# Softmax attention on one core: the negated row maxima as twelve more rows of the second scores' operands

## The reference, cut to what matters

```python
h = tok(x)                                  # embedding, 6 dilated causal convolutions, log-softmax
h = h + attn(layernorm(h), Q, E)            # causal linear attention, no softmax
h = h + ffn(layernorm(h), ...)              # the block below, B=8 sequences, T=256 rows, C=64
# in ffn: NH = 4 query heads, NKV = 2 key/value heads, HD = 16
q, k = rope(h @ wq.T), rope(h @ wk.T)
scores = einsum('bhtd,bhsd->bhts', q, k) / sqrt(HD)
scores = where(causal, scores, -1e30)
att = softmax(scores, axis=-1)
y = einsum('bhts,bhsd->bhtd', att, v)
x = x + y @ wo.T
# then rmsnorm, a router over 8 experts (top 2) and the experts' silu(x w1) * (x w3) @ w2
```

## Time and profile before

| what | value |
|---|---|
| median of 3 runs | 255.79 us (255.70 to 256.33) |
| profiled execution, its own time | 255.79 us |
| its span (first to last instruction) | 254.1 us |
| PE, DVE, ACT, POOL busy | 86%, 71%, 64%, 63% of the span |
| granted TensorE clock | 1.00 throughout |
| softmax attention, 118 to 172 us | PE 45.1, DVE 41.7, ACT 30.7, POOL 37.2 us busy of 54 |

### The profile page before, as it was taken

How to read it: one execution, slowest core, us unless ns; L and a number is a source line. 1 busy time by engine, 2 the same in 40 slices (tenths; PEclk the granted TensorE clock), 3 DMA queues, 4 the chain that set the end, 5 groups by cost and what they waited for, 6 DMA issues and landing times.

```text
span 254.1 us, 6618 instructions
## 1 busy us (share of the span) xinstructions
PE 219.6 (86%) x2460; PEld 150.8 (59%) x2468; DVE 179.4 (71%) x423; ACT 163.1 (64%) x294; POOL 160.0 (63%) x207
## 2 busy tenths in 40 slices
PE   8978879889898999997688888979799899889992
PEld 3644546367675785885566666754366466455661
DVE  4136657862578588578997687947977975999686
ACT  2478765679877497766545555568766578576670
POOL 6898201524467565378457888647789884876771
PEclk9999999999999999999999999999999999999999
DMA  2585300000000000000000000000000000010010
GB/s 43 138 186 123 70 3 3 3 1 0 3 0 3 0 0 3 1 4 0 3 0 3 0 3 3 1 4 0 3 4 0 3 22 3 0 23 3 0 25 22
DMA packets 7467, 4.48 MB, mean 18 GB/s; under 512 B 6500, under 2 KB 6796, under 8 KB 7436
## 3 DMA queue, kind: packets, MB, share of 16 engines
q1 hardware_dynamic: 7436, 4.06, 6.9%
HBM read 3.53 MB, written 0.52 MB: 16 GB/s over the span
## 4 chain that ended last, share of the span: by engine, by line
PE 50%; DVE 26%; ACT 9%; issue 9%; POOL 5%; DVEq 0%; ACTq 0%; POOLq 0%
PE bank L1416 48%; DVE nmx L1167 3%; DVE shared L1377 2%; DVE L L1344 1%; POOL shared L419 1%; ACT early L709 1%; DVE oT L1197 1%; DVE early L881 1%; PE bank L1642 1%; ACT qT L834 1%; DVE shared L995 1%; ACT early L576 1%; ACT qT L688 1%; DVE s L1214 1%; POOL qst L497 1%
## 5 line engine op out<-in xcount | busy, mean ns | idle before, releaser
L1416 PE MATMUL bank<-early 64*64 64x256 f32 (+5 forms) x556 | 56.7, 352 | 12.5 <-DVE early L881 3.1
L419 POOL TENSOR_TENSOR shared<-shared 128x512 f16<-128x512 f32 x44 | 51.3, 1166 | 17.1 <-ACT shared L819 14.4
L1416 PEld LDWEIGHTS bank<-early 64*64 64x64 f32 (+3 forms) x556 | 30.6, 126 | 30.5 <-issue 6.2
L1377 DVE SCALAR_TENSOR_TENSOR shared<-bank,qT 128x512 f32<-128x512 f32 x44 | 29.7, 687 | 12.4 <-ACT qT L834 10.5
L819 ACT CAST shared<-shared 128x512 f16<-128x512 f32 x44 | 27.0, 614 | 12.1 <-DVE shared L1377 12.1
L1416 PE MATMUL bank<-qT,shared 128*128 128x256 f32 x112 | 31.0, 387 | 3.0 <-DVE shared L995 3.0
L834 ACT ACTIVATE qT<-bank 128x512 f32<-128x512 f32 x44 | 26.3, 597 | 10.5 <-PE bank L1416 10.3
L504 POOL TENSOR_TENSOR oTx<-oT,oTx 128x512 f16<-128x512 f32 x16 | 19.3, 1209 | 18.9 <-ACT oTx L700 18.9
L349 POOL TENSOR_TENSOR stat<-stat,neghalf 128x4 f32<-128x4 f32 x14 | 14.2, 1015 | 26.0 <-DVE stat L966 21.6
L1416 PE MATMUL bank<-onehot,w3h 128*128 128x512 f16 x88 | 26.3, 380 | 3.6 <-DVE shared L1377 3.5
L1416 PE MATMUL bank<-onehot,w1h 128*128 128x512 f16 x88 | 26.2, 380 | 0.3 <-ACT qT L834 0.3
(11 more groups left out here) (247 smaller groups left out, 479.5 us busy)
## 6 DMA issues: line engine op xcount, KB each, us to landing
early<-in_tcn_w_dram SPq DMA_DIRECT2D x2, 320.0 KB, 4.2
w1s<-in_w1m_dram SPq DMA_DIRECT2D x2, 256.0 KB, 3.7
qT<-in_w3m_dram SPq DMA_DIRECT2D x2, 256.0 KB, 3.7
out_dram<-L SPq DMA_DIRECT2D x8, 64.0 KB, 1.7
qw<-in_attn_q_dram SPq DMA_DIRECT2D x2, 128.0 KB, 2.9
hTs<-in_w2m_dram SPq DMA_DIRECT2D x1, 256.0 KB
cos<-in_cos_t_dram SPq DMA_DIRECT2D x2, 96.0 KB, 2.9
sin<-in_sin_t_dram SPq DMA_DIRECT2D x2, 96.0 KB, 2.2
```

The lines of the kernel that those rows point to most:

```text
L419: nc.gpsimd.tensor_tensor(hhx[:, i, 1, :], hh[:, u % RING, :], hhx[:, i, 0, :], ALU.subtract).then_inc(S["lo_ready"], 1)
L1377: V_.scalar_tensor_tensor(hh[:, u % RING, :], bank[B_BANK[u % 2]][:, :], HH_SCALE / FFN_SCALE, sil[:, u % 2, :], ALU.mult, ALU.mult).then_ ...
L1416: return nc.tensor.matmul(out_, l_, r_, start=a, stop=z, skip_group_check=skip)
```

## The change

The twelve parts of the negated maxima (three for each of four heads) become rows 96 to 107 of `qkT`, under the 96 rows of the operands. In the key blocks these rows hold constants (`headsel`): ones in the six rows of the heads that share the key block, zeros in the others. In the query blocks they hold the parts of the one head, zero elsewhere. So one product over 108 rows gives the shifted score, and the products with `selh` go. `headsel` is built by GpSimd instead of `selh`; GpSimd fills the key rows in eight copies (`key_ones`) in the first four steps of the linear attention; the copy out of bank 0 moves from VectorE to ScalarE, becomes two scaled copies of 12 partitions x 512 elements, with the scale read from a column of `headsel`, and stands behind the last `probs` (and `stacked`) of a round.

```diff
-        qkT = early[0:96, ...
+        qkT = early[:, ...
-            link(nc.gpsimd.memset(selh[:, :, :], 1.0))
-            link(nc.gpsimd.affine_select(out=selh[:, :, :], ...
-            const(nc.gpsimd.affine_select(out=selh[:, :, :], ...
+            # headsel: two memsets, five affine_selects of one column, one tensor_scalar
+            def key_ones(i):
+                g4 = slice(4 * i, 4 * i + 4)
+                if i == 0:
+                    pool.wait_ge(S["shl_ready"], 1)
+                    pool.wait_ge(S["q_ps"], 1)
+                for kv in range(NKV):
+                    nc.gpsimd.tensor_copy(qkT[ROW_M:K_ROWS, g4, NH + kv, :], headsel[ROW_M:K_ROWS, kv:kv + 1].unsqueeze(2)
+                                          .to_broadcast([K_ROWS - ROW_M, 4, P])).then_inc(S["ones_ready"], 1)
+                    pool.wait_ge(S["ones_ready"], 2 * i + kv + 1)
...
+                if p == 0:
+                    key_ones(s)            # in the loop over tiles, behind low_rows(g - 1)
...
+            def max_out(b):                # ScalarE
+                act.wait_ge(S["nmT_ps"], b + 1)
+                src = bank[0][ROW_M:K_ROWS, 0:P].bitcast(bf16)...to_broadcast([K_ROWS - ROW_M, 2, 2, P])
+                for odd in range(2):
+                    r = nc.scalar.mul(qkT[ROW_M:K_ROWS, 2 * b:2 * b + 2, odd:NH:2, :], src,
+                                      headsel[ROW_M:K_ROWS, 2 + odd:3 + odd])
+                r.then_inc(S["nmT_ready"], 1)
             h_rows(2)
             second_copies()
+            max_out(0)
...
                 if (b, 2) in STACK_B:
                     stacked(STACK_B[b, 2])
+                max_out(b + 1)
...
-            def max_out(b):                # VectorE, with its two calls
...
-                        mm(ov_, qkT[:, 2 * b, NH + n_ // 2, :], qkT[:, 2 * b:2 * b + 2, n_, :], True, False)
-                        mm(ov_, selh[:, n_, :], nmT[:, b % 2, :, :], False, False)
+                        mm(ov_, qkT[0:K_ROWS, 2 * b, NH + n_ // 2, :], qkT[0:K_ROWS, 2 * b:2 * b + 2, n_, :], True,
+                           False)
...
-                        mm(ov_, selh[:, n_, :], nmT[:, b % 2, 1, :], False, False)
```

More of the change, by code:

```diff
@@ L22 @@
 NEG = -1e30
+ROW_M = 6 * HD
+K_ROWS = ROW_M + 3 * NH
 ATT_SCALE, FFN_SCALE, HH_SCALE = 64.0, 16.0, 4.0
@@ L57, in tower @@
         hid2 = early[:, NW + NX + 1024:NW + NX + 2048].rearrange("p (a c) -> p a c", a=PAIRS)
-        qkT = early[0:96, 0:TILES * 6 * P // 2].bitcast(bf16).rearrange("p (g n t) -> p g n t", n=6, t=P)
+        qkT = early[:, 0:TILES * 6 * P // 2].bitcast(bf16).rearrange("p (g n t) -> p g n t", n=6, t=P)
         bt = sb("bt", [P, 2 * LAYERS + 1])
@@ L78, in tower @@
         mask_s = sb("mask_s", [P, 4, P], bf16)
-        selh = sb("selh", [P, NH, P], bf16)
+        headsel = sb("headsel", [P, 4])
         neghalf = sb("neghalf", [P, 4])
@@ L330, in _, with row_select @@
                                               pattern=[[0, NH], [sgn, P]], channel_multiplier=-sgn))
-            link(nc.gpsimd.memset(selh[:, :, :], 1.0))
[L332 to L335, removed]
+            def row_select(col, first, fill):
+                c_ = headsel[:, col:col + 1]
+                link(nc.gpsimd.affine_select(out=c_, in_=c_, compare_op=ALU.is_ge, fill=fill, base=-first,
+                                             pattern=[[0, 1]], channel_multiplier=1))
+            link(nc.gpsimd.memset(headsel[:, 0:3], 0.0))
+            link(nc.gpsimd.memset(headsel[:, 1:2], 1.0))
+            row_select(0, ROW_M + 6, 1.0)
+            row_select(1, ROW_M + 6, 0.0)
+            row_select(2, ROW_M + 9, 1.0)
+            row_select(2, ROW_M + 6, 0.0)
+            row_select(2, ROW_M + 3, 1.0)
+            const(nc.gpsimd.tensor_scalar(headsel[:, 3:4], headsel[:, 2:3], -1.0, 1.0, ALU.mult, ALU.add))
             const(nc.gpsimd.memset(vaug[:, :, :, :], 1.0))
@@ L708, in stacked @@
                 act.wait_ge(S["stk_ps"], g + 1)
-                nc.scalar.copy(qkT[:, g, :, :].rearrange("p a b -> p (a b)"),
+                nc.scalar.copy(qkT[0:96, g, :, :].rearrange("p a b -> p (a b)"),
                                bank[stack_bank(g)][0:96, 0:384].bitcast(bf16)).then_inc(S["stk_ready"], 1)
@@ L784, in second_copies @@
                     nc.scalar.copy(d_[:, :, heads, dst, :], d_[:, :, heads, src, :]).then_inc(S["copies1_ready"], 1)
+            def max_out(b):
+                act.wait_ge(S["nmT_ps"], b + 1)
+                src = bank[0][ROW_M:K_ROWS, 0:P].bitcast(bf16).rearrange("p (a t) -> p a t", a=2).unsqueeze(2) \
+                    .to_broadcast([K_ROWS - ROW_M, 2, 2, P])
+                for odd in range(2):
+                    r = nc.scalar.mul(qkT[ROW_M:K_ROWS, 2 * b:2 * b + 2, odd:NH:2, :], src,
+                                      headsel[ROW_M:K_ROWS, 2 + odd:3 + odd])
+                r.then_inc(S["nmT_ready"], 1)
             h_rows(2)
             second_copies()
+            max_out(0)
             for b in range(B - 1):
@@ L1171, in row_max @@
                 src, r_ = nmx[:, 2 * b:2 * b + 2, :], nmr[:, b % 2, :, :]
-                d_ = nms[:, b % 2, :, 0:3 * NH].rearrange("p a (n k) -> p a n k", k=3)
+                d_ = nms[:, b % 2, :, ROW_M:K_ROWS].rearrange("p a (n k) -> p a n k", k=3)
                 if b >= 2:
@@ L1270, in _ @@
             last_centre()
-            max_out(0)
             last_bases()
@@ L1284, in _ @@
                     shares(b - 1)
-                if b + 1 < B:
-                    max_out(b + 1)
                 if b == 6:
@@ L1660, in scores_for_max @@
                     for n_ in range(NH):
-                        r = mm(o[:, P * n_:P * n_ + P], qkT[:, 2 * b, n_, :], qkT[:, 2 * b, NH + n_ // 2, :],
+                        r = mm(o[:, P * n_:P * n_ + P], qkT[0:96, 2 * b, n_, :], qkT[0:96, 2 * b, NH + n_ // 2, :],
                                False, n_ == NH - 1)
@@ L1685, in scores_shifted @@
                 if U == 0:
+                    pe.wait_ge(S["ones_ready"], 8)
                     pe.wait_ge(S["v_ready"], 2)
```

12 lines of the change are left out of this document (3 added, 9 removed).

## The result

The changed kernel takes 257.95 us (median of 13 executions, 255.97 to 258.77); the kernel before took 256.04 beside it (13 executions, 255.41 to 257.55). The ratio is 1.0055, interval 1.003 to 1.008: slower by half a per cent, where 255.4 us had been forecast. (The ratio is close to that of the means, 257.58 to 256.19; the medians are 1.91 us apart.) The thirteen times fall in two groups: five at 255.97 to 256.28, whose spans are 253.7 to 254.0, and eight at 257.89 to 258.77 with spans of 255.7 to 256.5. The profiled execution is of the second group, at 258.77.

What follows compares the result with a forecast made beforehand. No single engine was taken to bound the attention; GpSimd's chain and the last maxima copy set its waits. Against 255.79 us, 0.31 later minus 0.70 shorter products gave -0.39, so 255.4 us, range 253.9 to 256.4.

Steps and rivals of the forecast that it cites:

- Products removed: TensorE's shifted scores in the attention: 0.23 us less per scores_shifted, 5.5 in all; growing to 108 rows costs nothing.
- TensorE was not the bound: Rival that TensorE bounds the kernel, so all removed products count: 5.5 us off, 250.3 us, chance 0.04.
- Up to tile 12: GpSimd's second_split(3) chain starts about 0.45 us earlier (bounds 0.2 and 0.9), so tile 12 is stacked at 151.23, not 151.68.
- To the last maxima: From tile 12 to row_max(7): VectorE 0.65 us early, line 1178 ending at 163.43; max_rows(7) starts at 163.48.
- The last copy: ScalarE's pair behind probs(6, 2), 0.59 + 0.68 us: scores_shifted(7, 0) starts at 166.06, 0.31 later than before.
- The step that failed: Behind the last wait: three scores_shifted 0.70 us shorter, no longer waits between, TensorE entering the experts 0.4 us early.
- No rival of the prediction: Rivals: dearer copy pair (0.12), nothing left (0.16), cheaper tail or earlier start (0.14), TensorE the bound (0.04).
- the four signs: Wrong if copies cost over 1 us, GpSimd doesn't release tile 12, its chain starts over 1 us earlier, or earlier stages move.
- The other seven copies: On ScalarE, rounds before the last: about 1.27 us more a round, done before TensorE asks; the first ends 0.2 later, made up.

Runs made afterwards that it cites:

- the last copy first: Changed kernel with ScalarE's max_out(7) ahead of probs(6, 2), in round 6 alone: 255.83 us, ratio 0.9996 to the kernel before.
- a semaphore fewer: Changed kernel with max_out(7) ahead of probs(6, 2) and key_ones counting on bdS0_ready instead of its own semaphore: 255.47 us, ratio 0.9976.
- only the early waits filled: Changed kernel with unread 512-column products in TensorE's four early waits, none in the last: 258.16 us, ratio 1.0065.
- all waits filled: Changed kernel with unread 512-column products in TensorE's four early waits and eight in its last: 256.75 us, ratio 1.0018.
- last wait filled: Changed kernel with eight unread 512-column products on TensorE behind scores_shifted(6, 2), early waits unfilled: 257.23 us, ratio 1.0059.
- copies on VectorE: Changed kernel with its scaled copies as tensor_scalar in the old places on VectorE: 260.87 us, ratio 1.0188.
- selectors gone: Kernel before with the new constants and key rows, 64 selector products left out, VectorE's copy kept, nothing subtracted from the scores: 255.42 us, ratio 0.9981.
- copy kept: Changed kernel with VectorE's eight copies of the maxima kept beside ScalarE's, and ScalarE waiting for them: 258.45 us, ratio 1.0117.

## Why the prediction was wrong, point by point

**Products removed: right.** The stretch behind the last wait is 0.69 us shorter at full clock, forecast 0.70. Twelve more rows cost nothing. TensorE was not the bound.

**Up to tile 12: mechanism right, size not settled by one trace.** GpSimd's chain starts here, after:

```profile
133.81 0.40 POOL L354 CAST shlB<-qw 128x256 f16<-128x256 f32 x1 [1.72 <-issue]
```

It is 0.23 earlier than before, not 0.45: near the lower bound. But two kernels with the same order up to here, the one with the last copy first and the one with a semaphore fewer, start the chain at 133.61 and 133.52, 0.43 and 0.52 earlier than before, although their convolutions end 0.17 and 0.10 later.

**To the last maxima.** The last small instruction of the maxima, after:

```profile
163.62 0.18 DVE L1214 TENSOR_TENSOR ex<-nmr,ex 128x8 bf16<-128x8 f32 x1
```

It ends at 163.80: 0.28 earlier than before's 164.08, forecast 0.65 (163.43). In the two kernels just named it ends at 163.51 and 163.52, 0.57 and 0.56 earlier. What is missing here is within what two traces of the same code differ by.

**The last copy: price right, start 0.5 later than forecast.** The instructions that touch `headsel`, and ScalarE at the last maxima, after:

```profile
L816 ACT ACTIVATE early<-bank,headsel x16: 663/672/680, 120.9 to 165.8; 12x512 bf16<-12x512 bf16 x16
L370 POOL CAST early<-headsel x8: 607/610/692, 54.8 to 65.1; 12x512 bf16<-12x512 f32 x8
```

```profile
164.62 0.60 ACT L776 ACTIVATE qT<-bank 128x512 f32<-128x512 f32 x1 [0.44 <-PE bank L1443]
165.25 1.25 ACT L816 ACTIVATE early<-bank,headsel 12x512 bf16<-12x512 bf16 x2
```

672 ns for a copy (forecast 0.68), 610 ns for GpSimd's (0.61), and 0.76 from `max_rows(7)` to `probs(6, 2)`, as forecast. Two terms were off: `max_rows(7)` came at 163.86 instead of 163.48, since VectorE was less early, and the copy started 0.63 behind the exponential's start instead of 0.50. Together 0.51, and 0.50 is measured: 166.56 instead of 166.06.

**The step that failed** is the last of that paragraph: "Behind it come the last three `scores_shifted`, 3 x 0.23 = 0.70 shorter, with nothing between them that waits longer than before. TensorE enters the experts 0.4 us early". It took the durations behind the wait from a profile in which the wait was 0.50 us, and priced a wait of about 2 us, which the prediction itself named, at its length alone. Behind the wait, TensorE ran at half its clock: 5.65 us instead of 3.21, a loss of 2.44, all of it at the head of the experts. That the idle wait is a cause is shown by the pair with and without products in it, and that half the wait avoids the group of long times, by the last copy put first (none of 24 executions over 256.65, with the version of one semaphore fewer). It is not enough by itself: of the six traces with a last wait of 1.97 us or more, three fell behind it and three did not. No rival of the prediction spoke of the clock, and none of the four signs by which it was to be seen wrong came true: the copies cost 0.67, GpSimd releases tile 12, its chain starts less than 1 us earlier, and the stages before 118 us stay within 0.1. The Trainium skill, page "TensorE: Matmul & The Clock Gate", section "What's actually happening", says that TensorE's default state is the throttled one and that activity releases the throttle; the rows agree, 0.50 behind a wait and 1.00 some microseconds into the work. A longer wait in front of work that TensorE bounds ought to have been a rival; the rows above price it at 2.4 us.

**A second term was put at nothing**, ahead of the prediction: "what lies around it is taken as fixed". It is 0.5 us more, 0.58 between the two profiled executions.

**The sum again.** 255.4, plus 0.51 for the later start, 2.44 for the clock and 0.58 outside the span (258.77 - 256.5 = 2.27 in the profiled execution, 255.79 - 254.1 = 1.69 in that of before) gives 258.9; measured 258.77, since from `w1h` to the end it is 0.12 shorter. Without the fall it gives 256.5. Executions of this schedule that did keep the clock are the three short ones with only the early waits filled, 255.62 to 256.20, and the twelve with all waits filled, 255.79 to 257.24. (The changed kernel's own short group, 255.97 to 256.28, has mean clocks of 0.987 to 0.993.) So even with its clock kept this schedule gains nothing that can be told from the kernel before: what it saves, ScalarE's place for the last copy and the time outside the span take back.

**The other seven copies.** The first shifted scores started at 122.16 instead of 121.74, 0.4 later (0.2 forecast), and that is made up on the way, since tile 12 is early. But it is one more longer wait, and falls at 122 to 130 us came in five profiles: that of the changed kernel once more, and those of four edited ones (last wait filled, copies on VectorE, selectors gone, copy kept). What such a fall costs by itself was not isolated.

**Not settled.** Why the removal of VectorE's copies brings 0.2 to 0.5 us outside the span: the runs show that it goes with them, not by what. What decides, at the same wait, whether an execution loses the clock: in traces, waits of 1.97, 2.18 and 2.47 us passed at full clock, and 1.97 us did not in three. And why the copy on ScalarE began 0.63 behind the exponential and not 0.50.

## What to carry to other kernels

A wait of TensorE in front of a stretch that it bounds can cost more than its length, so when an edit lengthens one, price the stretch behind it at half clock as well, and look at the times of many executions, since the loss comes in some of them only. Where a small copy moves to another engine's queue, put it ahead of the work that nobody is waiting for: one place in ScalarE's order took the ratio to the kernel before from 1.0055 to 0.9996 here. And take the time outside the span from both kernels before comparing spans.

## What the runs showed of the hardware

- TensorE's granted clock fell to 0.50 behind waits of about 2 us in some executions of one and the same kernel and not in others; a fall at 166 us lasted 3.4 us in two traces and 6.8 in one, and cost 1.3, 1.5 and 2.4 us.
- Products that nobody reads, put into the waits, kept the mean clock at 0.994 or more in 12 of 12 executions.
- A scaled copy of 12 partitions x 512 from the banks to partitions 96 to 107 takes 672 ns on ScalarE and 488 ns on VectorE; the plain copy of 128 x 256 takes 369 ns on ScalarE and 280 on VectorE.
- The time between span and execution varies by 0.1 to 0.3 us within a kernel and differs between kernels: 1.66 to 1.79 before, 2.19 to 2.28 after.
- With the same code up to there, the convolutions ended at 39.78 us in one traced execution (copies on VectorE) and at 41.00 in another (all waits filled).
